# A softmax attention in periods of two key tiles, with values in three blocks, maxima in single banks, and every eighth unit of maxima folded by GpSimd

## The chip, the cores and the metric

The kernel runs on one core of a Trainium2 chip. The metric is the device time of one execution in microseconds (us); smaller is better. Five engines share the work: TensorE (PE in the profile, its weight loads PEld), VectorE (DVE), ScalarE (ACT), GpSimd (POOL), and SyncE (SP), which issues most DMAs.

## What is computed

Two transformer layers over 2 x 2048 tokens of width 256. Softmax attention with 16 heads of 16 stands in layer 0 and again in the last part of layer 1; between them lie a mixture of experts and a linear attention. The change touches softmax attention alone:

```python
q, k, v = x @ W_q.T, x @ W_k.T, x @ W_v.T          # each (B, L, 16 heads, 16); rope on q and k in layer 0
scores = einsum('blhd,bshd->bhls', q, k) / sqrt(16)
weights = softmax(scores, axis=-1)                  # over the 2048 keys
out = einsum('bhls,bshd->blhd', weights, v)
```

In layer 1 the same `softmax(q @ k.T) @ v` is computed from `x @ W_qkv + b_qkv`, and the result of the experts is added to it.

## The kernel before

`softmax_attention` is called twice; each call is one stage of the kernel. A stage goes through 32 **groups** (2 batches x 4 groups of four heads x 4 pieces of 512 queries; `n` counts them), so there are 64 groups in all. A group goes through 16 tiles of 128 keys (`u`). For each key tile and each of the four heads TensorE forms a **score** (128 keys x 512 queries, contraction over 50 rows) into one of `SB` = 3 PSUM banks (L835), ScalarE takes the exponential of it into `probs` (L905), and TensorE multiplies that with the values, 17 columns for each head, into `o_ps` (L850). The four heads' value products stand in four column strips of the array and run side by side; each is recorded as two MATMULs. The last of the 17 columns is the sum by which the result is divided.

So that the exponential doesn't overflow, every query's maximum score is needed before its group begins. It is a row of q itself (the shift rows), so it must be there ahead. For that TensorE forms the scores a second time, turned over (128 queries x 512 keys, L823, `maximum`), in **units** of one PSUM bank. VectorE reduces two units at once (L924, `max_take`, 128x1024 to 128x2) into `part_max`. There are 64 units in a group. They run `LEAD` = 8 key tiles ahead of the group that they are for. When all are there, four small steps on VectorE (`row_maxima`, L278 to L291) make the row that SP stores and loads into q.

A score reads rows 0 to 49 or 64 to 113 of the array, by the head, and a unit of maxima reads the other half: such a **pair** of score and maximum runs side by side. TensorE's order is written out by hand. In a key tile it is twice this **round**: a block of values of 256 columns for the tile before, then a pair, then a second pair. At `u` = 1 the first block is put off, which makes a run of four pairs and then 512 columns of values, so that VectorE has time to turn the finished result out of `o_ps` (`turn_result`, L930). `divide` (L934, L938) follows at `u` = 2.

The engines are tied by counting semaphores. Score c waits for exponential c-3. A pair of maxima waits until its two banks (of 2 x 2) were reduced. A block of values waits for the tile's four exponentials. The exponentials of a tile wait for the values of two tiles earlier, since `probs` has two buffers. Within one engine everything is in order.

GpSimd zeroes a DRAM buffer in the first stage (ten DMAs, after the first group). In the second it gathers the experts' rows with 64 indirect DMAs (L780), weighs and adds them (L786 to L793), and adds the finished rows (L800, L802). SP loads queries and keys ahead and stores results.

## Time and profile before

| what | value |
|---|---|
| median of 3 runs | 3513.06 us (3509.66 to 3520.32) |
| profiled execution, its own time | 3515.13 us |
| its span, first to last instruction | 3513.4 us |
| mean granted TensorE clock | 0.969 of full |
| PE busy | 3376.8 us (96%) |
| DVE busy | 3031.7 us (86%) |
| ACT busy | 2546.2 us (72%) |
| POOL busy | 514.1 us (15%) |
| the two attention stages | from 180 to 1446 us and from 2236 to about 3500 us of the span |

Busy time counts an instruction from its start to its end. The next one on the same engine can start before the end of the one ahead, so on DVE and ACT the distance between starts in a row of waiting work (called pitch below) is shorter than the duration, and an engine that reads 100% busy may still have room.

### The profile page before, as it was taken

How to read it: one execution, taken by the hardware profiler on the slowest of the kernel's cores; microseconds unless marked ns; L12 is line 12 of the kernel's file. 1: busy time of each engine (PE TensorE's matmuls, PEld its weight loads, DVE VectorE, ACT ScalarE, POOL GpSimd, SP SyncE). 2: the span in 40 equal slices, each digit the busy share in tenths (PEclk: the TensorE clock that was granted, in tenths of full speed). 3: DMA queues.
4: the chain of work that ended last, by engine and by line, in shares of the span. 5: the costliest groups of instructions: out<-in, count | busy, mean ns of one | idle time of the engine just before them, and what ended most of it. 6: DMA issues, size and time to landing. Idle time of an engine off the chain costs nothing. (4 is left out here: it accounts for less than half of the span.)

```text
span 3513.4 us, 74309 instructions
## 1 busy us (share of the span) xinstructions
PE 3376.8 (96%) x29745; PEld 1550.6 (44%) x29746; DVE 3031.7 (86%) x3971; ACT 2546.2 (72%) x4700; POOL 514.1 (15%) x405
## 2 busy tenths in 40 slices
PE   8999999999999999878999889999999999999998
PEld 5533333333333333567777657533333333333333
DVE  8889999999999998364787565599999999999992
ACT  4178888888888888533333224688888888888887
POOL 4410000000000000053321142155410010000001
PEclk9689999999999999989999989999999999999999
DMA  8451220202021200335010385513121231203001
GB/s 268 131 163 25 34 39 15 43 17 39 15 39 28 32 14 6 126 132 187 28 33 12 128 256 182 133 42 64 44 44 29 42 63 27 43 16 39 15 18 46
DMA packets 306962, 233.29 MB, mean 66 GB/s; under 512 B 205592, under 2 KB 257721, under 8 KB 301971
## 3 DMA queue, kind: packets, MB, share of 16 engines
q1 hardware_dynamic: 290308, 179.45, 22.3%
q0 software_dynamic: 14832, 47.79, 4.1%
q8 instruction: 221, 3.62, 0.5%
q10 hardware_dynamic: 1504, 1.64, 0.1%
q14 instruction: 97, 0.79, 0.1%
HBM read 126.49 MB, written 102.76 MB: 65 GB/s over the span
## 5 line engine op out<-in xcount | busy, mean ns | idle before, releaser
L905 ACT ACTIVATE att_l_probs<-att_l_s_ps 128x512 f32<-128x512 f32 x4096 | 2214.6, 595 | 312.1 <-PE att_l_s_ps L835 246.8
L924 DVE TENSOR_REDUCE att_in_part_max<-att_l_max_ps 128x2 f32<-128x1024 f32 x1952 | 2327.5, 1217 | 13.7 <-PE att_l_max_ps L823 13.1
L850 PE MATMUL att_l_o_ps<-att_l_probs,att_l_v_sb 128*17 128x256 f32 x16384 | 1273.6, 386 | 2.9 <-DMA att_l_v_sb<-v_rows 1.6
L835 PE MATMUL att_l_s_ps<-att_in_q_sb,att_in_k_sb 50*128 50x512 f32 x2048 | 759.8, 447 | 9.0 <-DVE att_l_o_ps L941 9.0
L835 PE MATMUL att_l_s_ps<-att_in_q_sb,att_l_k_sb 50*128 50x512 f32 x2048 | 741.5, 448 | 0.1
L823 PE MATMUL att_l_max_ps<-att_l_k_sb,att_in_q_sb 50*128 50x512 f32 x2048 | 725.4, 444 | 0.7 <-DVE att_in_part_max L924 0.7
L823 PE MATMUL att_l_max_ps<-att_in_k_sb,att_in_q_sb 50*128 50x512 f32 x1856 | 666.5, 449 | 0.8 <-DVE att_in_part_max L924 0.8
L850 PEld LDWEIGHTS att_l_o_ps<-att_l_probs,att_l_v_sb 128*17 128x17 f32 x16384 | 278.6, 95 | 724.6 <-issue 382.9
L835 PEld LDWEIGHTS att_l_s_ps<-att_in_q_sb,att_in_k_sb 50*128 50x128 f32 x2048 | 312.2, 186 | 443.9 <-ACT att_l_probs L905 415.7
L835 PEld LDWEIGHTS att_l_s_ps<-att_in_q_sb,att_l_k_sb 50*128 50x128 f32 x2048 | 307.7, 184 | 434.1 <-ACT att_l_probs L905 397.2
L823 PEld LDWEIGHTS att_l_max_ps<-att_l_k_sb,att_in_q_sb 50*128 50x128 f32 x2048 | 291.2, 184 | 6.9 <-DVE att_in_part_max L924 6.9
L823 PEld LDWEIGHTS att_l_max_ps<-att_in_k_sb,att_in_q_sb 50*128 50x128 f32 x1856 | 266.6, 186 | 6.7 <-DVE att_in_part_max L924 6.5
L1175 POOL MEMSET post_ones<- 128x128 bf16 x1 | 0.2, 205 | 1217.8 <-POOLq L71 1217.8
L800 POOL TENSOR_TENSOR att<-att,all_gates 128x1024 f32<-128x1024 f32 x7 | 16.6, 2375 | 852.4 <-DMA att<-att_rows 852.4
L930 DVE STREAM_TRANSPOSE att_l_o_sb<-att_l_o_ps 128x512 f32<-128x512 f32 x64 | 45.2, 706 | 102.2 <-PE att_l_o_ps L850 102.2
L1736 ACT ACTIVATE lin_o_sb<-lin_o_ps 128x512 f32<-128x512 f32 x32 | 19.1, 598 | 99.3 <-PE lin_o_ps L1631 99.3
L780 POOL DMA_INDIRECT att_l_got<-tile_out,all_get_at x64 | 64.6, 1010 | 152.7 <-ACT att_l_probs L905 149.6
L1820 DVE TENSOR_TENSOR lin_masked<-lin_qk_ps,all_triu 128x1024 f32<-128x1024 f32 x64 | 75.2, 1217 | 9.6 <-PE lin_qk_ps L1622 9.6
L266 DVE TENSOR_REDUCE att_in_part_max<-ffn_qk_ps 128x2 f32<-128x1024 f32 x48 | 56.5, 1217 | 30.6 <-PE ffn_qk_ps L257 30.6
L2108 PE MATMUL ffn_v_ps<-ffn_w_exp,ffn_hT 128*128 x320 | 82.1, 385 | 0.0
L2015 POOL DMA_INDIRECT slot_rows<-ffn_z_all,all_get_at x64 | 62.8, 981 | 96.0 <-DVE all_get_at L2282 77.1
L1178 POOL DMA_INDIRECT slot_rows<-next_z_all,post_put_at x64 | 62.5, 976 | 86.1 <-DVE all_get_at L1472 68.1
(262 smaller groups left out, 2778.7 us busy)
## 6 DMA issues: line engine op xcount, KB each, us to landing
att_in_q_sb<-q_hi SPq DMA_DIRECT2D x256, 64.0 KB
slot_rows<-att_l_zeros POOLq DMA_DIRECT2D x10, 1024.0 KB, 15.7
ffn_parts<-slot_rows SPq DMA_DIRECT2D x40, 256.0 KB, 3.1
tile_out<-ffn_parts SPq DMA_DIRECT2D x40, 256.0 KB, 2.2
att_in_q_sb<-q_lo SPq DMA_DIRECT2D x128, 72.0 KB
att_l_v_sb<-v_rows SPq DMA_DIRECT2D x16, 544.0 KB, 15.9
att_in_k_sb<-k_hi SPq DMA_DIRECT2D x32, 256.0 KB, 9.1
att_l_k_sb<-k_hi SPq DMA_DIRECT2D x32, 256.0 KB, 10.0
```

The lines of the kernel that those rows point to most:

```text
L266: nc.vector.reduce_max(ai.part_max[:, k // MAXI, k % MAXI], ps[:, k % 2 * 2:k % 2 * 2 + 2], AX.X).then_inc(ai.slot_taken, 1)
L780: nc.gpsimd.indirect_dma_start(out=got[:, k, t], out_offset=None, in_=io.tile_out, in_offset=bass.IndirectOffsetOnAxis(ap=m.get_at[:, b, k ...
L823: ins = nc.tensor.matmul(max_ps[:, r, half], q_sb[rows, j % QR, pair, tile * P:(tile + 1) * P], k_sb[j // GPB % 2][rows, pair, part * G:(p ...
L835: nc.tensor.matmul(s_ps[:, c % SB], k_sb[j // GPB % 2][rows, pair, u * P:(u + 1) * P], q_sb[rows, j % QR, pair], start=True, stop=True).th ...
L850: last = nc.tensor.matmul(o_ps[32 * h:32 * h + AUG, cols], v_sb[:, j // GPB % 2, u, h * AUG:(h + 1) * AUG], probs[:, u % 2, h, cols], star ...
L905: nc.scalar.activation(probs[:, u % 2, h], s_ps[:, c % SB], ACT.Exp, scale=float(HD) ** -0.5).then_inc(exp_done, 1)
L924: nc.vector.reduce_max(part_max[:, j % 2, k], max_ps[:, r], AX.X).then_inc(slot_taken, 1)
L930: nc.vector.transpose(o_sb[:].rearrange("p k c -> p (k c)"), o_ps[:]).then_inc(o_copied, 1)
L1178: nc.gpsimd.indirect_dma_start(out=io.slot_rows, out_offset=bass.IndirectOffsetOnAxis(ap=put_at[:, b, k, t:t + 1], axis=0), in_=m.z_all[:, ...
L1820: nc.vector.tensor_tensor(masked[:, t % 2, banks].rearrange("p r e n -> p (r e) n"), qk_ps[:, banks].rearrange("p r (e n) -> p (r e) n", n=P),
L2015: nc.gpsimd.indirect_dma_start(out=io.slot_rows, out_offset=bass.IndirectOffsetOnAxis(ap=m.get_at[:, b, k, t:t + 1], axis=0), in_=z_all[:, ...
L2108: last = nc.tensor.matmul(out_ps[:, i % 2, t], slot_hT[:, i % 2, kh, t * P:(t + 1) * P], w_exp[:, kh, ds(experts[t] * D, D)], start=False, ...
```

## The change

- **Periods.** Two key tiles make a period (`w`, 8 in a group). In it TensorE does 8 pairs and three blocks of values in place of four: 3 pairs, values 0:320 of the tile before; 2 pairs, its values 320:512; 3 pairs, values 0:512 of the period's first tile. Period 0 of a group has two blocks of 512 columns, behind 3 and behind 5 pairs. `probs` gets a third buffer (`PB`).
- **Maxima in single banks.** The eight units of a period go through four single banks. VectorE takes units 0, (1, 2), 3, 4 and (5, 6): three reduces of one bank and two of two banks.
- **Unit 7 by another way.** ScalarE copies it from PSUM to SBUF behind the period's eight exponentials (L959, `unit_sb`). GpSimd folds its upper half onto the lower (L779 to L783: high minus low, maximum with 0, plus low) into `folded`, 256 wide. VectorE reduces four folded units at once (L993, `take_folds`), twice in a group: in period 4 and in period 5, each time behind unit 0. The four steps of `row_maxima` follow in period 5, `divide` moves to period 1.
- **GpSimd's other work** is now interleaved with the folds, one piece a period.

Core of the diff (the new helpers `zero_rows`, `gather`, `add_experts`, `add_result` hold the loops' old bodies and are left out):

```diff
+PB = 3
+STEP_TILES = 2
+STEPS_G = KT // STEP_TILES
+UNITS = 4 * STEP_TILES
+MB = 4
+TAKES = ((0,), (1, 2), (3,), (4,), (5, 6))
+COPIED = UNITS - 1
+HB = 4
+FOLDED = MAXI // GPB
+ROUNDS = ((3, 0, 320), (2, 320, 512), (3, 0, 512))
+RESULT_STEP, ROWMAX_STEP = 1, LEAD // STEP_TILES + 1
-        max_ps = pb("max_ps", [P, 2, 2, G])
+        max_ps = pb("max_ps", [P, MB, G])
...
+            def reduce_unit(p):
+                g, k, half = unit_of(p // STEPS_G, p % STEPS_G, COPIED)
+                pool.wait_ge(unit_copied, p + 1)
+                low, high = unit_sb[:, p % HB, 0:G // 2], unit_sb[:, p % HB, G // 2:G]
+                nc.gpsimd.tensor_tensor(high, high, low, ALU.subtract).then_inc(fold_step, 1)
+                pool.wait_ge(fold_step, 2 * p + 1)
+                nc.gpsimd.tensor_scalar(high, high, 0.0, None, ALU.max).then_inc(fold_step, 1)
+                pool.wait_ge(fold_step, 2 * p + 2)
+                nc.gpsimd.tensor_tensor(folded[:, g % 2, k // GPB], low, high, ALU.add).then_inc(unit_reduced, 1)
...
+                behind, held = divmod(UNITS * p + i - MB, UNITS)
+                if behind >= 0:
+                    if held == COPIED:
+                        pe.wait_ge(unit_copied, behind + 1)
+                    else:
+                        pe.wait_ge(units_taken, behind * len(TAKES) + TAKE_OF[held] + 1)
...
+                    for r, (count, c0, c1) in enumerate(ROUNDS):
+                        products(n, w, pair, count)
+                        pair += count
+                        values(n, STEP_TILES * w - (r < 2), c0, c1)
...
+            def copy_unit(p):
+                act.wait_ge(unit_ready, UNITS * p + COPIED + 1)
+                if p >= HB:
+                    act.wait_ge(unit_reduced, p - HB + 1)
+                nc.scalar.activation(unit_sb[:, p % HB], max_ps[:, COPIED % MB], ACT.Copy).then_inc(unit_copied, 1)
...
+            for n in range(STEPS):
+                for w in range(STEPS_G):
+                    for t in range(len(TAKES)):
+                        take_units(n, w, t)
+                        if w == ROWMAX_STEP - 1 and t == 0 and 0 < n < STEPS - 1:
+                            take_folds(n + 1, 0)
+                        if w == ROWMAX_STEP and n + 1 < STEPS:
+                            if t == 0:
+                                take_folds(n + 1, 1)
+                                dve.wait_ge(folds_taken, 2 * n + 1)
+                                dve.wait_ge(units_taken, period_of(n, LEAD // STEP_TILES) * len(TAKES))
+                            else:
+                                row_maxima(nc, dve, ai, n + 1, n + 1, t - 1, FIRST)
```

How this moves the work on two engines. First TensorE, before, in the middle of a group of the first stage: two key tiles (`att_l0_s_ps` is a score, `att_l0_max_ps` a unit of maxima, `att_l0_o_ps` the values).

```order
L850 MATMUL att_l0_o_ps<-att_l0_probs,att_l0_v_sb 17x256 x4
L835 MATMUL att_l0_s_ps<-att_in0_q_sb,att_in0_k_sb0 128x512
L823 MATMUL att_l0_max_ps<-att_in0_k_sb0,att_in0_q_sb 128x512 x2
L835 MATMUL att_l0_s_ps<-att_in0_q_sb,att_in0_k_sb0 128x512
L850 MATMUL att_l0_o_ps<-att_l0_probs,att_l0_v_sb 17x256 x4
L835 MATMUL att_l0_s_ps<-att_in0_q_sb,att_in0_k_sb0 128x512
```

The same engine after the change, one whole period:

```order
L895 MATMUL att_l0_s_ps<-att_in0_q_sb,att_in0_k_sb0 128x512
L885 MATMUL att_l0_max_ps<-att_in0_k_sb0,att_in0_q_sb 128x512 x2
L895 MATMUL att_l0_s_ps<-att_in0_q_sb,att_in0_k_sb0 128x512 x2
L885 MATMUL att_l0_max_ps<-att_in0_k_sb0,att_in0_q_sb 128x512
L910 MATMUL att_l0_o_ps<-att_l0_probs,att_l0_v_sb 17x320 x4
L885 MATMUL att_l0_max_ps<-att_in0_k_sb0,att_in0_q_sb 128x512
L895 MATMUL att_l0_s_ps<-att_in0_q_sb,att_in0_k_sb0 128x512 x2
L885 MATMUL att_l0_max_ps<-att_in0_k_sb0,att_in0_q_sb 128x512
L910 MATMUL att_l0_o_ps<-att_l0_probs,att_l0_v_sb 17x192 x4
```

TensorE now goes from pairs to values and back three times in two key tiles, and not four times.

VectorE before, where a group's row maxima are made, up to where the result is turned:

```order
L278 TENSOR_REDUCE att_in0_row_max<-att_in0_part_max 128x8 x2
L924 TENSOR_REDUCE att_in0_part_max<-att_l0_max_ps 128x2
L282 CAST att_in0_max_parts<-att_in0_row_max 128x16
L924 TENSOR_REDUCE att_in0_part_max<-att_l0_max_ps 128x2
L285 TENSOR_TENSOR att_in0_max_parts<-att_in0_row_max,att_in0_max_parts 128x16
L924 TENSOR_REDUCE att_in0_part_max<-att_l0_max_ps 128x2
L291 STREAM_TRANSPOSE att_in0_max_cols<-att_in0_max_parts 128x32
L924 TENSOR_REDUCE att_in0_part_max<-att_l0_max_ps 128x2 x13
L930 STREAM_TRANSPOSE att_l0_o_sb<-att_l0_o_ps 128x512
```

VectorE after, from the first take of a group's period 5 to the first of period 6 (L984 takes units, L993 folded units; another L993 stands in the same place of period 4):

```order
L984 TENSOR_REDUCE att_in0_part_max<-att_l0_max_ps 128x1
L993 TENSOR_REDUCE att_in0_part_max<-att_l0_folded 128x4
L984 TENSOR_REDUCE att_in0_part_max<-att_l0_max_ps 128x2
L278 TENSOR_REDUCE att_in0_row_max<-att_in0_part_max 128x8 x2
L984 TENSOR_REDUCE att_in0_part_max<-att_l0_max_ps 128x1
L282 CAST att_in0_max_parts<-att_in0_row_max 128x16
L984 TENSOR_REDUCE att_in0_part_max<-att_l0_max_ps 128x1
L285 TENSOR_TENSOR att_in0_max_parts<-att_in0_row_max,att_in0_max_parts 128x16
L984 TENSOR_REDUCE att_in0_part_max<-att_l0_max_ps 128x2
L291 STREAM_TRANSPOSE att_in0_max_cols<-att_in0_max_parts 128x32
L984 TENSOR_REDUCE att_in0_part_max<-att_l0_max_ps 128x1
```

A reduce of folded units, 4 x 256 elements long, now stands in front of the take that the row maxima follow, and the four small steps lie behind single takes and not 16 tiles' even pairs.

## Rows read from the trace of the kernel before

**Rows 1.** The page, part 1: busy time of each engine and its instructions

```profile
PE 3376.8 (96%) x29745; PEld 1550.6 (44%) x29746; DVE 3031.7 (86%) x3971; ACT 2546.2 (72%) x4700; POOL 514.1 (15%) x405
```

**Rows 2.** Busy time by stretch, first stage: PE, PEld, DVE, ACT, POOL, clock, DMA

```profile
208.00:1370.00 1162.00, 1162.00 (x11334) 422.01 (x11332) 1160.65 (x1182) 1022.04 (x1889) 5.36 (x10) 1.00 0.19 35
```

**Rows 3.** L930 alone, one a group, in two stretches: durations in ns, starts

```profile
L930 DVE STREAM_TRANSPOSE att_l_o_sb<-att_l_o_ps x30: 705/705/707, 229.5 to 1371.8; 128x512 f32<-128x512 f32 x30
...
L930 DVE STREAM_TRANSPOSE att_l_o_sb<-att_l_o_ps x3: 707/717/718, 1371.8 to 1444.1; 128x512 f32<-128x512 f32 x3
```

**Rows 4.** Timeline of PE in a steady round: start us, us, engine, line

```profile
712.25 0.63 PE L850 MATMUL att_l_o_ps<-att_l_probs,att_l_v_sb 128*17 128x256 f32 x8
712.81 0.49 PE L835 MATMUL att_l_s_ps<-att_in_q_sb,att_l_k_sb 50*128 50x512 f32 x1
...
713.14 0.38 PE L835 MATMUL att_l_s_ps<-att_in_q_sb,att_l_k_sb 50*128 50x512 f32 x1
713.47 0.63 PE L850 MATMUL att_l_o_ps<-att_l_probs,att_l_v_sb 128*17 128x256 f32 x8
```

**Rows 5.** Timeline at a group's tile 1: four pairs, then 512 columns of values

```profile
699.78 2.45 DVE L924 TENSOR_REDUCE att_in_part_max<-att_l_max_ps 128x2 f32<-128x1024 f32 x2
...
701.46 0.50 PE L835 MATMUL att_l_s_ps<-att_in_q_sb,att_l_k_sb 50*128 50x512 f32 x1
...
701.80 0.62 PE L835 MATMUL att_l_s_ps<-att_in_q_sb,att_l_k_sb 50*128 50x512 f32 x2
...
702.28 0.49 PE L823 MATMUL att_l_max_ps<-att_l_k_sb,att_in_q_sb 50*128 50x512 f32 x2
...
703.13 1.06 PE L850 MATMUL att_l_o_ps<-att_l_probs,att_l_v_sb 128*17 128x256 f32 x16
...
704.12 0.49 PE L835 MATMUL att_l_s_ps<-att_in_q_sb,att_l_k_sb 50*128 50x512 f32 x1
```

**Rows 6.** Timeline of ACT: two exponentials back to back

```profile
709.59 1.08 ACT L905 ACTIVATE att_l_probs<-att_l_s_ps 128x512 f32<-128x512 f32 x2 [0.21 <-PE att_l_s_ps L835]
```

**Rows 7.** Timeline of DVE around a group's result

```profile
820.32 0.70 DVE L930 STREAM_TRANSPOSE att_l_o_sb<-att_l_o_ps 128x512 f32<-128x512 f32 x1
820.95 4.58 DVE L924 TENSOR_REDUCE att_in_part_max<-att_l_max_ps 128x2 f32<-128x1024 f32 x4
825.46 0.23 DVE L934 RECIPROCAL att_l_inv<-att_l_o_sb 128x16 f32<-128x16 f32 x1
...
826.07 4.61 DVE L924 TENSOR_REDUCE att_in_part_max<-att_l_max_ps 128x2 f32<-128x1024 f32 x4
```

**Rows 8.** Timeline of DVE around the row maxima

```profile
800.81 0.27 DVE L278 TENSOR_REDUCE att_in_row_max<-att_in_part_max 128x8 f32<-128x32 f32 x2
801.00 1.22 DVE L924 TENSOR_REDUCE att_in_part_max<-att_l_max_ps 128x2 f32<-128x1024 f32 x1
802.13 0.17 DVE L282 CAST att_in_max_parts<-att_in_row_max 128x16 fp32r<-128x16 f32 x1
```

**Rows 9.** Timeline of PE behind a `divide`: score, then its late unit

```profile
630.31 0.49 PE L835 MATMUL att_l_s_ps<-att_in_q_sb,att_in_k_sb 50*128 50x512 f32 x1
...
630.46 0.58 PE L823 MATMUL att_l_max_ps<-att_l_k_sb,att_in_q_sb 50*128 50x512 f32 x2
```

**Rows 10.** Groups of instructions on POOL: count, then busy us and mean ns

```profile
L448 POOL TENSOR_TENSOR qkv_parts<-qkv_whole,qkv_parts 128x512 fp32r<-128x512 f32 x32 | 40.1, 1276 | 54.4 <-ACT qkv_parts L535 54.4
...
L457 POOL TENSOR_SCALAR qkv_prod<-qkv_prod 128x1024 f32<-128x1024 f32 x2 | 5.6, 2785 | 0.2
```

**Rows 11.** Timelines of DVE and of POOL in the second stage, row maxima

```profile
2418.07 0.27 DVE L278 TENSOR_REDUCE att_in_row_max<-att_in_part_max 128x8 f32<-128x32 f32 x2
...
2420.81 1.42 DVE L285 TENSOR_TENSOR att_in_max_parts<-att_in_row_max,att_in_max_parts 128x16 fp32r<-128x16 f32 x1
...
2417.34 2.39 POOL L788 TENSOR_TENSOR att_l_got<-att_l_got 128x1024 f32<-128x1024 f32 x1
2419.80 2.39 POOL L790 TENSOR_TENSOR att_l_got<-att_l_got,all_gates 128x1024 f32<-128x1024 f32 x1
```

More of the change, by code:

```diff
@@ new lines, in _ @@
+            for p in range(PERIODS):
+                reduce_unit(p)
+                if zero_slots and ZERO_STEP <= p < ZERO_STEP + B * ROWS_B * D // P // ZEROS:
+                    zero_rows(p - ZERO_STEP)
+                if last and 1 <= p <= B * GPB * (GATHERS + ADDS):
+                    i, s = divmod(p - 1, GATHERS + ADDS)
+                    if s < GATHERS:
+                        gather(i, s)
+                    else:
+                        add_experts(i, s - GATHERS)
+                if last:
+                    for i in range(RESULTS):
+                        if p - ADD_AT[i] in (0, 1):
+                            add_result(i, p - ADD_AT[i])
@@ L821, in maximum @@
+                behind, held = divmod(UNITS * p + i - MB, UNITS)
+                if behind >= 0:
+                    if held == COPIED:
+                        pe.wait_ge(unit_copied, behind + 1)
+                    else:
+                        pe.wait_ge(units_taken, behind * len(TAKES) + TAKE_OF[held] + 1)
                 pair, tile, part = maximum_parts(k)
                 rows = slice(half * HROWS, half * HROWS + XROWS)
[L823 to L824 removed]
@@ L825, in maximum @@
-                if half == 0:
-                    ins.then_inc(slot_ready, 1)
+                nc.tensor.matmul(max_ps[:, i % MB], q_sb[rows, j % QR, pair, tile * P:(tile + 1) * P],
+                                 k_sb[j // GPB % 2][rows, pair, part * G:(part + 1) * G], start=True, stop=True).then_inc(unit_ready, 1)
             def scores(n, j, u, h):
@@ L897, in _, with products @@
-            for part in range(2):
-                values(STEPS - 1, NB - 1, KT - 1, NIT - 1, part)
+            def products(n, w, first, count):
+                for pair in range(first, first + count):
+                    row, second = divmod(pair, 2)
+                    c = 2 * row + second
+                    u, h = STEP_TILES * w + c // HG, c % HG
+                    if second:
+                        maximum(n, w, c)
+                        scores(n, n % NB, u, h)
+                    else:
+                        scores(n, n % NB, u, h)
+                        maximum(n, w, c)
@@ L916, in _ @@
+            for n in range(STEPS):
+                for u in range(KT):
+                    for h in range(HG):
+                        if h == 0 and n * KT + u >= PB:
+                            act.wait_ge(pv_done, n * KT + u - PB + 1)
+                        exps(n, u, h)
+                    if u % STEP_TILES == STEP_TILES - 1 and period_of(n, u // STEP_TILES) < PERIODS:
+                        copy_unit(period_of(n, u // STEP_TILES))
             if last:
@@ L921, in _, with take_units, take_folds @@
         def _(dve):
-            def max_take(used, r, j, k):
-                dve.wait_ge(slot_ready, used + 1)
-                nc.vector.reduce_max(part_max[:, j % 2, k], max_ps[:, r], AX.X).then_inc(slot_taken, 1)
+            def take_units(n, w, t):
+                p, units = period_of(n, w), TAKES[t]
+                if p >= PERIODS:
+                    return
+                g, k, half = unit_of(n, w, units[0])
+                first = 2 * k + half
+                dst = part_max[:, g % 2, first:first + 1] if len(units) == 1 else part_max[:, g % 2, first:first + 4:3]
+                banks = max_ps[:, units[0] % MB:units[0] % MB + len(units)]
+                dve.wait_ge(unit_ready, UNITS * p + units[-1] + 1)
+                nc.vector.reduce_max(dst, banks, AX.X).then_inc(units_taken, 1)
+            def take_folds(g, part):
+                periods = period_of(g - 1, LEAD // STEP_TILES * part)
+                dve.wait_ge(unit_reduced, periods)
+                _, k, half = unit_of(0, 0, COPIED)
+                at = slice(part * FOLDED // 2, (part + 1) * FOLDED // 2)
+                first = 2 * (GPB * at.start + k % GPB) + half
+                dst = part_max[:, g % 2, first:2 * GPB * at.stop:2 * GPB]
+                nc.vector.reduce_max(dst, folded[:, g % 2, at], AX.X).then_inc(folds_taken, 1)
             def turn_result(n):
```

213 lines of the change are left out of this document (92 added, 121 removed).

## The prediction

> **What bounds the kernel now.** I read the page first, then busy time by stretch, then the timelines of the engines in one attention stage. PE is busy for 96% of the span and DVE for 86% [rows 1]; in the first stage both are busy all the time, at the full clock [rows 2]. So the reader has to ask which of them really has no room. Thirty turns of the result lie from 229.5 to 1371.8 us: 29 groups at 39.39 us [rows 3]. A steady round on PE goes value block 712.25, first pair 712.81, second pair 713.14, next block 713.47 [rows 4]: 1.22 us, 32 of them 39.0 us. Nothing in it is late. DVE's reduce of two units takes 1.22 us, but four that had work waiting stand at a pitch of (4.58 - 1.22) / 3 = 1.12, or 1.13 with 4.61 [rows 7]. 32 at 1.13 are 36.2, and with turn (0.63), divide (0.61) [rows 7] and row maxima (0.19 for the first step, 0.07 for the second [rows 8], and I take 0.1 each for the last two, 0.46 in all) 37.9 us a group. ACT has a pitch of 1.08 - 0.59 = 0.49 us [rows 6], 64 of them 31.4. So **PE is the bound, by its own work**, DVE is 3% under it, ACT 20%.
>
> **What PE's round is made of.** A block of 256 columns takes 0.56 us up to the next pair, one of 512 without a break 703.13 to 704.12 = 0.99 [rows 4, 5]. So a column costs 0.43 / 256 = 0.0017 us and a turn from values to pairs 0.12. In the run of four pairs the first pair holds 0.34, while the third starts 0.62 - 0.39 = 0.23 behind the second [rows 5]; the last pair before values holds 0.33. A pair thus costs 0.23 inside a run, with 0.10 more at each end of it. Every turn there and back costs some 0.33 us and works on nothing.
>
> In the Trainium skill, "TensorEngine Tiling (Array Packing)", Tiling Modes, Key Properties, says that a change of tiling mode drains TensorE. The trace agrees: the 0.1 us at each change.
>
> **The change on PE.** Runs of 3, 2 and 3 pairs: 0.34 + 0.23 + 0.33 = 0.90, 0.67, 0.90, together 2.47. Blocks of 320, 192 and 512 columns: 0.12 + 0.54 = 0.66, 0.45, 0.99, together 2.10. A period is 4.55 us, against 4 x 1.22 = 4.88. 8 periods are 36.4 us, **2.6 us a group less** if nobody else is late.
>
> **The change on DVE.** A take of one unit isn't in the trace. Half of a reduce's elements are worth 1.22 - 0.70 = 0.52 (against the turn of 512 elements [rows 7]); its pitch is then 1.13 - 0.52 = 0.61, its duration 0.70. Bounds: 0.57 (half of 1.13) and 0.63 (the turn's pitch). A period: 3 x 0.61 + 2 x 1.13 = 4.09, 8 of them 32.7. A reduce of folded units reads 1024 elements from SBUF: 1.13, not below the 1.04 that two times 0.52 give. Two of them, with the old 1.7 for turn, divide and maxima, make 36.7 us a group. So the ceiling on both engines is near 36.5, and the question is what they lose to each other.
>
> **Where they meet.** Count from a period's first pair. Units 0, 1, 2 are there at 0.53, 0.77 and 1.00, unit 3 at 2.1 and 5 and 6 at 3.4. DVE starts its takes at 0.53, 1.14, 2.27, 2.88 and 3.49. From the end of a reduce to PE's start are 0.05 (699.78 + 2.45 to 702.28 [rows 5]). The take of units 1, 2 ends at 2.36, and PE wants their bank at 2.66: 0.25 to spare. That of unit 3 ends at 2.97, PE wants it at 3.23: 0.20. That of 5, 6 ends at 4.71, PE wants it at 4.55 + 0.34 = 4.89: **0.12**. DVE is then free at 4.62 and the next unit 0 comes at 5.08, so DVE idles 0.46 a period, but it can't work ahead in it. Whatever is put on DVE in a period beyond 0.12 us moves PE, if it is put behind unit 0. Before the change such a pair was wanted 0.40 after it was free (the reduce that starts at 713.57 is done at 714.79, and its banks are wanted at 713.47 + 1.22 + 0.56 = 715.25); a divide of 0.61 then held one unit up by 0.15 [rows 9].
>
> The lumps of a group:
> - Period 4: 1.13 - 0.12 = 1.01.
> - Period 5: fold 1.13, and 0.19 + 0.07 + 0.1 of the row maxima ahead of the last take: 1.49 - 0.12 = 1.37.
> - Period 1: divide, 0.61 - 0.12 = 0.49.
> - Period 0: it has one turn of PE less (4.2 us), but unit 3 is taken behind the result's turn, from 2.90 to 3.60; its bank is wanted by pair 8. That starts at 3.65, values follow at 4.0 and end at 5.0 to 5.1: 0.5 over a common period.
>
> Sum 3.4. Where PE waits inside a run of pairs its pipeline fills again, 0.1 as at a run's start: up to six places, I take 0.4. ACT has nine operations a period, 9 x 0.49 = 4.4 of 4.55 (the copy priced as an exponential of the same shape): its room falls from 20% to 3%. The next period's first exponential is 0.1 late, and pair 8, which waits for exponential 4, loses some 0.02; 0.1 a group. **36.4 + 3.4 + 0.4 + 0.1 = 40.3**, and with 0.1 for GpSimd (next) 40.4 us a group, 1.0 more than now.
>
> **GpSimd.** Two-input 512 elements take 1.28, one-input 1024 2.79 [rows 10], two-input 1024 2.39 [rows 11]: for 256 about 0.7, 0.8 and 0.7, 2.3 us a period of 4.55, in a ring of four copies; the extra work of the second stage fits beside. Nobody waits for the folds as such. But while POOL worked on SBUF, DVE's subtraction of 16 elements (L285) took 1.42 us, and ended when POOL's operation did (2419.80 + 2.39 = 2422.19), while the reduces at 2418.07 weren't longer than elsewhere [rows 8, 11]. POOL is now at work half of each period in both stages. Open to it are L282, L285 and the product in `divide`, each by at most one operation, 0 to 0.8 us; by my times the row maxima miss POOL's three operations and the product meets the last. I take 0.1 a group; 0 and 1.5 stay as ends.
>
> The Trainium skill, "GPSIMD Engine Reference", Key points, says that GpSimd shares its SBUF interfaces with VectorE and contends with instructions that have two SBUF inputs or run in a two-port mode. That rule speaks against this change: the page and the row name the same steps. It gives no price; the sum with the row's bounds would be 0 to 1.5 us a group.
>
> **The rest.** 61 groups' worth carry maxima: 61 x 1.0 = 61 us more. The last 1.5 groups of each stage have none (two groups take 1444.1 - 1371.8 = 72.3 us [rows 3]); there ACT's pitch is the floor (3.95 for a period's eight) and one turn fewer gives 0.2 to 0.5 a period: 24 periods, 8 us less. The zeroing DMAs and gathers move to other times of POOL, whose queue nobody waits for; SP's queue keeps its order. Sum: 3515 + 61 - 8 = 3568 for the profiled execution; it was 2 us over the median, so about **3565 us**.
>
> **Rivals.**
> 1. *The lumps are absorbed.* For it: the units stand in four separate banks, and 0.46 us of idle is in each period; the room of 0.12 rests on differences of rows, and if single takes cost 0.57 and the rest is 0.1 better, each of the four lumps costs 0.2 less and no refill. Against it: the idle time lies before unit 0, the lumps behind it. Wholly absorbed, DVE bounds at 36.7: 3515 - 61 x 2.7 - 8 = 3342. Half absorbed (2 us a group less than forecast) it is 38.4: 3447. A chance of 0.27.
> 2. *GpSimd's hold on SBUF* becomes the dear part: it must reach L285, L282 and the product in most groups, 1.5 us a group in place of 0.1: 3565 + 85 = 3650. It decides once POOL's three operations last beyond 3.6 us of a period. For it: the one row of 1.42; against it: POOL's pieces are now a quarter as long. 0.10.
> 3. *It comes out even:* lumps of 2.4 in place of 3.4 and all else as forecast, 39.4 a group: 3507. 0.15.
> 4. *ScalarE is the bound:* if the copy takes 0.2 us more than an exponential, a period is 4.65 at least, but waits for DVE then shrink; 0.1 a period, 0.5 a group in all: 3595. 0.08. A table load for each copy (the change not doing what it says) is out: the program has one load per stage, as before.
>
> The forecast itself, lumps between 2.9 and 4.1 a group, has 0.40, and gives 3535 to 3610.
>
> **Range and chances.** 0.3% is about what a measurement of this kernel can tell. Faster 0.27 (rival 1), same 0.15 (rival 3), slower 0.58 (forecast, 2 and 4). The range takes in the forecast, rivals 3 and 4, and the half of rival 1 down to 3440, and reaches toward rival 2 at 3625. The likeliest case's own range is 3535 to 3610.
>
> **What would show it.** PE periods of 4.55 us in periods 2, 3, 6 and 7, with blocks and runs as priced; single takes at a pitch of 0.61; gaps on PE of 0.9 before unit 5 in periods 4 and 5, released by DVE; about 40.4 us from turn to turn. It is wrong if DVE has no idle time before unit 0, if the gaps in periods 4 and 5 are under 0.5, or if steady periods differ from 4.55 by over 0.1.

## The result, and the profile after

The changed kernel takes 3609.62 us (median of 4 runs, 3608.14 to 3612.86). The kernel before took 3511.36 in the same series (4 runs, 3508.97 to 3520.32). The ratio is 1.0273, with an interval of 1.0256 to 1.0291: slower, by some 98 us where 52 were forecast, inside the range of 3440 to 3625 and at the upper edge of the likeliest case. The profiled execution is the one of 3608.14 us (span 3606.4, mean granted clock 0.97).

The page after, part 1:

```profile
PE 3325.1 (92%) x25137; PEld 1540.8 (43%) x25138; DVE 2931.1 (81%) x4581; ACT 2717.8 (75%) x5188; POOL 1646.5 (46%) x1877
```

Busy time by stretch in the first attention stage and in the second (columns as in [rows 2]):

```profile
208.00:1370.00 1162.00, 1093.63 (x8862) 402.71 (x8859) 1070.54 (x1422) 1063.94 (x2045) 530.27 (x691) 1.00 0.19 35
2236.00:3440.00 1204.00, 1127.08 (x9000) 435.47 (x8998) 1063.98 (x1406) 1080.26 (x2076) 703.81 (x793) 1.00 0.23 44
```

In [rows 1] PE was busy for 96% of the span and in [rows 2] for all of the first stage. Now it is idle for 68 us of the same 1162, DVE for 91 and ACT for 98, at the same full clock. Nobody is full: the three engines wait for each other. Who waits for whom is in the page's part 5 (busy us, mean ns, then idle time before the group and its releaser):

```profile
L984 DVE TENSOR_REDUCE att_in_part_max<-att_l_max_ps 128x1 f32<-128x512 f32 (+1 forms) x2440 | 2072.9, 896 | 200.8 <-PE att_l_max_ps L885 194.0
...
L885 PE MATMUL att_l_max_ps<-att_l_k_sb,att_in_q_sb 50*128 50x512 f32 x2048 | 728.1, 444 | 73.3 <-DVE att_in_part_max L984 70.3
...
L885 PE MATMUL att_l_max_ps<-att_in_k_sb,att_in_q_sb 50*128 50x512 f32 x1856 | 662.8, 447 | 64.2 <-DVE att_in_part_max L984 61.3
```

PE's idle time lies before the units of maxima and is ended by DVE's takes; DVE's lies before its takes and is ended by PE. The turns of the result, against [rows 3]:

```profile
L999 DVE STREAM_TRANSPOSE att_l_o_sb<-att_l_o_ps x28: 704/706/707, 267.1 to 1372.2; 128x512 f32<-128x512 f32 x28
```

(1372.2 - 267.1) / 27 = 40.93 us a group, against 39.39. To place this inside a group I took, from the records of PE, the time from one period's first score to the next one's, as a mean over 27 groups of the first stage (w is the period; a group is the sum; in the kernel before a period is two key tiles).

| us | w0 | w1 | w2 | w3 | w4 | w5 | w6 | w7 | group |
|---|---|---|---|---|---|---|---|---|---|
| before | 5.09 | 4.88 | 5.04 | 4.88 | 4.88 | 4.87 | 4.87 | 4.87 | 39.39 |
| forecast (refills and small terms apart) | 5.05 | 5.04 | 4.55 | 4.55 | 5.56 | 5.92 | 4.55 | 4.55 | 40.4 |
| after | 5.06 | 5.35 | 4.78 | 4.68 | 5.58 | 5.90 | 4.92 | 4.67 | 40.93 |

The whole difference of 93 us between the profiled executions: the 29 groups between a stage's first and thirtieth turn give 44.9 and 44.6, together 89.5; the last two groups of each stage 2 x 1.96 = 3.9; the part of a stage from its first score to its first turn -4.4 and -0.4; what lies between and around the stages 4.4.

A steady period (w7) on PE, against [rows 4]:

```profile
669.38 0.50 PE L895 MATMUL att_l_s_ps<-att_in_q_sb,att_in_k_sb 50*128 50x512 f32 x1
...
670.27 0.73 PE L910 MATMUL att_l_o_ps<-att_l_probs,att_l_v_sb 128*17 128x320 f32 x8
670.94 0.50 PE L885 MATMUL att_l_max_ps<-att_l_k_sb,att_in_q_sb 50*128 50x512 f32 x1
...
671.60 0.52 PE L910 MATMUL att_l_o_ps<-att_l_probs,att_l_v_sb 128*17 128x192 f32 x8
672.05 0.50 PE L885 MATMUL att_l_max_ps<-att_l_k_sb,att_in_q_sb 50*128 50x512 f32 x1
...
672.62 0.39 PE L885 MATMUL att_l_max_ps<-att_l_k_sb,att_in_q_sb 50*128 50x512 f32 x1
672.64 0.50 PE L895 MATMUL att_l_s_ps<-att_in_q_sb,att_in_k_sb 50*128 50x512 f32 x1
673.07 1.05 PE L910 MATMUL att_l_o_ps<-att_l_probs,att_l_v_sb 128*17 128x512 f32 x8
674.05 0.49 PE L895 MATMUL att_l_s_ps<-att_in_q_sb,att_l_k_sb 50*128 50x512 f32 x1
```

Read the starts. The first run of three pairs takes 670.27 - 669.38 = 0.89, the block of 320 columns 0.67, the run of two 0.66, the block of 192 0.45, the long block 0.98: all as priced. Only the second run of three takes 1.02 in place of 0.90. Its last score starts a little behind its unit of maxima (672.64, not 672.62), and the values follow 0.43 behind it and not 0.33. What that score waits for stands under experiment 4.

The timeline of DVE around the folds of periods 4 and 5, then that of PE in period 4 (in brackets the idle time before and its releaser):

```profile
653.56 0.69 DVE L984 TENSOR_REDUCE att_in_part_max<-att_l_max_ps 128x1 f32<-128x512 f32 x1 [0.53 <-PE att_l_max_ps L885]
654.16 1.21 DVE L993 TENSOR_REDUCE att_in_part_max<-att_l_folded 128x4 f32<-128x1024 f32 x1
655.29 3.54 DVE L984 TENSOR_REDUCE att_in_part_max<-att_l_max_ps 128x2 f32<-128x1024 f32 x4
659.14 0.69 DVE L984 TENSOR_REDUCE att_in_part_max<-att_l_max_ps 128x1 f32<-128x512 f32 x1 [0.31 <-PE att_l_max_ps L885]
659.75 1.21 DVE L993 TENSOR_REDUCE att_in_part_max<-att_l_folded 128x4 f32<-128x1024 f32 x1
```

```profile
655.21 0.52 PE L910 MATMUL att_l_o_ps<-att_l_probs,att_l_v_sb 128*17 128x192 f32 x8
656.56 0.50 PE L885 MATMUL att_l_max_ps<-att_l_k_sb,att_in_q_sb 50*128 50x512 f32 x1 [0.83 <-DVE att_in_part_max L984]
```

DVE idles 0.53 us, takes unit 0, then reads the folded units for 655.29 - 654.16 = 1.13, and only then starts on units 1 and 2. PE has no room for unit 5 until they are read: 655.21 to 656.56 is 1.35 where 0.45 is the usual.

Period 6 holds no fold and still lasts 4.92. Its second pair waits for the take of units 5 and 6 of period 5, which the small steps of the row maxima have made late:

```profile
663.68 1.21 DVE L984 TENSOR_REDUCE att_in_part_max<-att_l_max_ps 128x2 f32<-128x1024 f32 x1
664.95 0.72 PE L895 MATMUL att_l_s_ps<-att_in_q_sb,att_in_k_sb 50*128 50x512 f32 x2
```

The take ends at 664.89 and the pair starts at 664.95, 0.48 behind the first one (664.47) where 0.34 is the usual: 0.14 of waiting, and 0.10 until PE is back at its pace, since the third pair follows 0.34 later and not 0.23.

### The profile page after: what moved, and what is told of

Same layout as the page of the kernel before. It is cut to its first block and busy times, and to the rows that moved or that the text cites. A ratio compares the mean times of both kernels' runs of the same rounds, so it can differ in the third digit from the quotient of the medians.

```text
span 3606.4 us, 68202 instructions
## 1 busy us (share of the span) xinstructions
PE 3325.1 (92%) x25137; PEld 1540.8 (43%) x25138; DVE 2931.1 (81%) x4581; ACT 2717.8 (75%) x5188; POOL 1646.5 (46%) x1877
## 5 line engine op out<-in xcount | busy, mean ns | idle before, releaser
L952 ACT ACTIVATE att_l_probs<-att_l_s_ps 128x512 f32<-128x512 f32 x4096 | 2158.2, 598 | 229.4 <-PE att_l_s_ps L895 206.5
L984 DVE TENSOR_REDUCE att_in_part_max<-att_l_max_ps 128x1 f32<-128x512 f32 (+1 forms) x2440 | 2072.9, 896 | 200.8 <-PE att_l_max_ps L885 194.0
L910 PE MATMUL att_l_o_ps<-att_l_probs,att_l_v_sb 128*17 128x512 f32 (+2 forms) x11776 | 1169.5, 469 | 1.1 <-DMA att_l_v_sb<-v_rows 1.0
L779 POOL TENSOR_TENSOR att_l_unit_sb<-att_l_unit_sb 128x256 f32<-128x256 f32 x488 | 358.4, 734 | 1081.4 <-ACT att_l_unit_sb L959 1080.9
L885 PEld LDWEIGHTS att_l_max_ps<-att_l_k_sb,att_in_q_sb 50*128 50x128 f32 x2048 | 330.2, 184 | 379.8 <-DVE att_in_part_max L984 202.8
L781 POOL TENSOR_SCALAR att_l_unit_sb<-att_l_unit_sb 128x256 f32<-128x256 f32 x488 | 413.0, 846 | 42.8
L910 PEld LDWEIGHTS att_l_o_ps<-att_l_probs,att_l_v_sb 128*17 128x17 f32 x11776 | 195.1, 95 | 462.0 <-issue 427.1
L783 POOL TENSOR_TENSOR att_l_folded<-att_l_unit_sb 128x256 f32<-128x256 f32 x488 | 356.5, 731 | 40.6
L959 ACT ACTIVATE att_l_unit_sb<-att_l_max_ps 128x512 f32<-128x512 f32 x488 | 301.1, 617 | 0.0
L993 DVE TENSOR_REDUCE att_in_part_max<-att_l_folded 128x4 f32<-128x1024 f32 x122 | 147.7, 1211 | 5.4 <-POOL att_l_folded L783 5.4
```

The costliest lines, as they stand in the source:

```text
L779: nc.gpsimd.tensor_tensor(high, high, low, ALU.subtract).then_inc(fold_step, 1)
L781: nc.gpsimd.tensor_scalar(high, high, 0.0, None, ALU.max).then_inc(fold_step, 1)
L783: nc.gpsimd.tensor_tensor(folded[:, g % 2, k // GPB], low, high, ALU.add).then_inc(unit_reduced, 1)
L885: nc.tensor.matmul(max_ps[:, i % MB], q_sb[rows, j % QR, pair, tile * P:(tile + 1) * P], k_sb[j // GPB % 2][rows, pair, part * G:(part + 1 ...
L910: last = nc.tensor.matmul(o_ps[32 * h:32 * h + AUG, c0:c1], v_sb[:, j // GPB % 2, u, h * AUG:(h + 1) * AUG], probs[:, (n * KT + u) % PB, h ...
L952: nc.scalar.activation(probs[:, (n * KT + u) % PB, h], s_ps[:, c % SB], ACT.Exp, scale=float(HD) ** -0.5).then_inc(exp_done, 1)
```

## Experiments

All times are of the first attention stage unless said otherwise. Four runs stand beside one run of the kernel before of 3522.02 us (the first four here), the rest beside 3515.76 (median of 9), the last beside 3513.83. Experiments 5 and 6 were run five times, the others once, so a difference of some 10 us between their totals says little; the times of the periods say more.

**1. Folds made small.** VectorE reads 16 of each 256 folded elements; the number and places of its instructions stay. What is left out is most of the folded values.

```diff
-                nc.vector.reduce_max(dst, folded[:, g % 2, at], AX.X)
+                nc.vector.reduce_max(dst, folded[:, g % 2, at, 0:16], AX.X)
```

> Edit: VectorE's two reduces of folded units read 4 x 16 elements in place of 4 x 256, so part of the keys is left out of the row maxima; everything else as in the changed kernel (40.91 us a group). Theory A (what is put on DVE behind a period's unit 0 moves PE, because DVE can't use its idle time ahead of unit 0): the two folds of 1.13 us cost PE about 1.0 us each and 0.1 to 0.2 of refill, so a group takes 38.6 to 38.9 us, the time is 3470 to 3490 us, and period 4 is as long as period 3 (4.68 us in place of 5.58). Theory B (ScalarE's ninth operation and GpSimd's hold on SBUF set the time, the folds lie in DVE's idle time): within 0.2 us of 40.9 a group, 3600 us.

Measured: 3510.61 us, 39.03 a group, both longer than expected. Period 4 went from 5.58 to 4.68, period 5 from 5.90 to 4.90, all others stayed. The reduce went from 1211 to 211 ns (DVE's instructions by form):

```profile
L993 DVE TENSOR_REDUCE att_in_part_max<-att_l_folded 128x4 f32<-128x64 f32 x57 | 12.0, 211 | 0.0
```

1.0 us less on DVE gave 0.91 and 0.99 of PE's time. So the two folds, where they stood, are what made the kernel slower: without them it stands at the kernel before. In the second stage a group took 39.59, though its median periods are those of the first stage; five of its periods 6 last 6.9 to 9.7 us, of the kind shown at experiment 5.

**2. Folds moved behind the period's last take.** Nothing is left out.

```diff
+                        if w == ROWMAX_STEP - 3 and t == len(TAKES) - 1 and 0 < n < STEPS - 1:
+                            take_folds(n + 1, 0)
+                        if w == ROWMAX_STEP - 1 and t == len(TAKES) - 1 and n + 1 < STEPS:
+                            take_folds(n + 1, 1)
```

> Edit: the same two reduces of folded units, at full size, stand behind the last take of periods 2 and 4 in place of behind the first take of periods 4 and 5. DVE's work is the same to the element. Theory A: behind the last take DVE has its idle time of about 0.5 us, so a fold makes it late by 0.6 and PE by 0.3 to 0.5, not 1.0: 39.6 to 40.0 us a group, 3530 to 3555 us. Theory C (DVE's summed work decides, wherever it stands): no change, 40.9 a group, 3608 us.

Measured: 3541.77 us, 39.60 a group, as theory A said; w3 is 4.94, w4 4.76, w5 5.12. The fold now begins when DVE would have gone idle:

```profile
642.22 4.20 DVE L984 TENSOR_REDUCE att_in_part_max<-att_l_max_ps 128x1 f32<-128x512 f32 x5 [0.31 <-PE att_l_max_ps L885]
646.34 1.21 DVE L993 TENSOR_REDUCE att_in_part_max<-att_l_folded 128x4 f32<-128x1024 f32 x1
647.46 1.81 DVE L984 TENSOR_REDUCE att_in_part_max<-att_l_max_ps 128x1 f32<-128x512 f32 x2
```

A group is 0.57 us longer than with the shrunken folds of experiment 1, where it was 1.90 longer with the folds behind unit 0. The gap before unit 0 is real room, and the place decides what a step on DVE costs.

**3. One folded unit a period.** Eight reduces of 256 elements, each behind its period's last take.

```diff
+                        if t == 4 and 0 < period_of(n, w) <= PERIODS:
+                            take_fold(period_of(n, w) - 1)
```

> Edit: each folded unit is reduced by itself (128x256), one in every period, behind the last take; eight reduces of 256 elements in place of two of 1024. DVE's work rises by eight fixed parts of some 0.07 us. Theory A: a reduce of 256 elements has a pitch of 0.33 us, less than the idle 0.5, so the folds cost PE nothing: 38.6 to 38.9 us a group, as with the folds shrunk, 3470 to 3490 us; that would be below the kernel before. Theory C: 8 x 0.07 = 0.5 us a group more, 41.4, 3640 us.

Measured: 3490.76 us, 38.77 a group; w4 and w5 are both 4.68, w6 4.89. The group is as expected, the total 1 us over. Shortest, median and longest duration of the folds:

```profile
L990 DVE TENSOR_REDUCE att_in_part_max<-att_l_folded x488: 395/407/421, 194.1 to 3421.2; 128x1 f32<-128x256 f32 x163
```

Eight reduces hold DVE longer than two (its busy time is 2934.2 against 2931.1 us), and the profiled execution is 117 us shorter. This is the cut of the work that fits the gap.

**4. The cut of the values at 288.** ROUNDS becomes (3, 0:288), (2, 288:512), (3, 0:512).

> Edit: the values of the second tile are cut 0:288 and 288:512, not 0:320 and 320:512; so scores 3 and 4 start 0.05 us earlier, and the period's other work stands still. Theory D (the steady period of 4.67 us, forecast 4.55, is 0.12 too long since pair 8's score waits for exponential 4, some 0.03 us, and the pipeline that runs dry costs 0.1 more): periods 3 and 7 fall to 4.56 to 4.60, a group to 40.2 to 40.6 us, 3565 to 3590 us. Rival (ScalarE's nine operations at their pitch fill the period, 9 x 0.49 = 4.4 and its waits): periods 3 and 7 stay at 4.67, 3608 us.

Measured: 3593.59 us, 40.83 a group; the steady periods are 4.62, 0.05 less where 0.08 to 0.12 were expected. On PE, the last run of three in a steady period:

```profile
671.36 0.50 PE L885 MATMUL att_l_max_ps<-att_l_k_sb,att_in_q_sb 50*128 50x512 f32 x1
...
671.93 0.39 PE L885 MATMUL att_l_max_ps<-att_l_k_sb,att_in_q_sb 50*128 50x512 f32 x1
672.33 1.05 PE L910 MATMUL att_l_o_ps<-att_l_probs,att_l_v_sb 128*17 128x512 f32 x8
```

The run takes 0.97 now, between 1.02 and 0.90. What is left of the wait shows in the weight loads of this run (PEld):

```profile
671.47 0.45 PEld L885 LDWEIGHTS att_l_max_ps<-att_l_k_sb,att_in_q_sb 50*128 50x128 f32 x2
671.90 0.18 PEld L895 LDWEIGHTS att_l_s_ps<-att_in_q_sb,att_in_k_sb 50*128 50x128 f32 x1
```

In the changed kernel the last one stands at:

```profile
672.64 0.18 PEld L895 LDWEIGHTS att_l_s_ps<-att_in_q_sb,att_in_k_sb 50*128 50x128 f32 x1
```

The last score waits for exponential 4, the period's fifth. Counted from the period's start, as means over 27 groups, this exponential ends at 3.16 (3.21 in the changed kernel), the score's weights are loaded at 3.21 (3.26), and the unit beside it has had its own since 3.04 in both. The score now starts together with its unit (3.24 both), and the values still follow 0.40 behind it: 0.43 in the changed kernel, 0.33 in a run that waits for nothing. So the exponential moved with the scores by the full 0.05, and the period with it. The load stays 0.17 late, and of the 0.12 there is 0.07 left, which goes with this late load and not with a pair that starts apart. A cut still earlier, which would test that, wasn't run.

This run's mean contains two disturbed groups (18 and 24), each 1.3 us longer at a granted clock of 0.50; the median periods add up to 40.70 a group, against 40.90 in the changed kernel.

**5. Experiments 3 and 4 together, with the small steps put last.** The reciprocal goes behind the last take of period 1, the product behind that of period 2.

```diff
+                        if n > 0 and w == 1 and t == len(TAKES) - 1:
+                            invert(n - 1)
+                        if n > 0 and w == 2 and t == len(TAKES) - 1:
+                            scale_result(n - 1, n - 1)
```

> Edit: as the kernel with one folded unit a period (38.77 us a group in the first stage, 3490.8 us), and the values' cut at 288, and the divide taken apart: the reciprocal behind the last take of period 1, the product behind that of period 2, where GpSimd's three operations are over. Theory A (idle time of DVE lies between the last take and the next unit 0, some 0.5 us, and steps that fit there are free): the 0.8 us that periods 1 and 2 lose to the divide fall to 0.2, the product takes 0.43 in place of 0.69 us, the cut gives 0.05 in five periods: 37.6 to 38.1 us a group, 3405 to 3445 us, below the kernel before by 2 to 3%. Rival (the divide's lump is only moved: recovered elsewhere, 3.3% of work is work): 38.6 to 38.8 us a group, 3480 us.

Measured in five rounds: 3432.71 us (3426.99 to 3443.62), a ratio to the kernel before of 0.9771 (0.9752 to 0.9790), so 2.3% faster. A group is 37.84: 5.06, 4.70, 4.68, 4.62, 4.63, 4.64, 4.88, 4.62. DVE in periods 0 to 2:

```profile
612.45 0.41 DVE L990 TENSOR_REDUCE att_in_part_max<-att_l_folded 128x1 f32<-128x256 f32 x1
612.78 0.24 DVE L1000 RECIPROCAL att_l_inv<-att_l_o_sb 128x16 f32<-128x16 f32 x1
613.02 4.15 DVE L984 TENSOR_REDUCE att_in_part_max<-att_l_max_ps 128x1 f32<-128x512 f32 x5
617.08 0.41 DVE L990 TENSOR_REDUCE att_in_part_max<-att_l_folded 128x1 f32<-128x256 f32 x1
617.41 0.41 DVE L1006 TENSOR_TENSOR att_l_o_div<-att_l_o_sb,att_l_inv 128x256 f32<-128x256 f32 x1
617.74 4.14 DVE L984 TENSOR_REDUCE att_in_part_max<-att_l_max_ps 128x1 f32<-128x512 f32 x5
```

The steps follow each other without a gap, and PE doesn't wait for them beyond 0.1. Period 6 keeps its 4.88: the small steps of the row maxima still stand ahead of a take.

In the second stage 29 groups take 1113.6 us against 1097.7 in the first. The median periods are the same; four periods 6 last 8.08, 9.77, 8.87 and 6.05 us. Just ahead of each, L285, a step of the row maxima, is held by one of GpSimd's operations for the experts (1.33 to 1.82 us in place of 0.16). In the longest:

```profile
2441.44 2.37 POOL L813 TENSOR_TENSOR all_x_res<-all_x_res,att_l_got 128x1024 f32<-128x1024 f32 x1
2442.04 1.81 DVE L285 TENSOR_TENSOR att_in_max_parts<-att_in_row_max,att_in_max_parts 128x16 fp32r<-128x16 f32 x1
```

Busy time by stretch there (columns as in [rows 2]):

```profile
2443.00:2445.00 2.00, 0.07 (x2) 0.00 (x0) 2.00 (x3) 0.83 (x2) 1.91 (x3) 1.00 0.01 4
2445.00:2449.00 4.00, 3.96 (x24) 1.20 (x24) 3.22 (x6) 2.05 (x4) 2.24 (x3) 0.52 0.15 38
```

The take of units 5 and 6 comes late by the hold, PE is busy for 0.07 of 2 us, and in the four behind them its granted clock is 0.52, near the lower level of 1.2 GHz. The period loses 4.9 us for a hold of 1.7. Three of the four long periods have such a stretch. This is the hold that rival 2 of the prediction is about; with what follows it, it costs some 16 us in this version.

**6. The turn one take later,** behind unit 3 and no longer ahead of it, on top of experiment 5 (`t == 2` for `t == 1`).

> Edit: as e5_small_steps_last, with the turn of the result behind the take of unit 3 and not in front of it. Theory A: unit 3's bank is free 0.6 us earlier and pair 8 no longer waits for it, but then waits for exponential 4, so period 0 falls by 0.1 us or less, from 5.05; 6 us less in all than e5_small_steps_last. Rival: the values behind it wait for the turn, which ends 0.6 us later, period 0 grows by up to 0.3 us, 18 us more.

Measured in five rounds: 3444.31 us (3438.40 to 3450.55), 0.9802 (0.9785 to 0.9819). w0 fell by 0.07 to 4.99, as the early wait for unit 3 says, but w1 rose by 0.18 to 4.88. The step's time came back in the next period, and more of it: neither expectation had that. A group is 0.11 longer in the first stage (37.95) and 0.02 in the second; of the 11 us between the two profiled executions 7.5 lie outside the attention stages. So the move gains nothing, and it costs some 3 us rather than 11.

**7. GpSimd made short.** It subtracts and clamps 16 elements and copies the lower half, so that the upper half of unit 7 is left out. (Of the diff, one of three such lines.)

```diff
-                nc.gpsimd.tensor_tensor(high, high, low, ALU.subtract).then_inc(fold_step, 1)
+                tiny = high[:, 0:16]
+                nc.gpsimd.tensor_tensor(tiny, tiny, low[:, 0:16], ALU.subtract).then_inc(fold_step, 1)
```

> Edit to the changed kernel: GpSimd copies only the lower half of the unit (128x256, one input) and does two steps of 16 elements, in place of three operations of 256; the other half of every eighth unit is left out of the maxima. POOL's chain in a period falls from 2.45 to some 1.3 us; nothing else is changed. Theory E (the divide's product, 0.69 us in place of 0.42, is held by GpSimd's third operation, and that moves PE): the product is back at 0.42 to 0.43, periods 1 and 2 together fall by 0.25, group 40.65 us, 3590 us. Rival (the product is longer for another reason, its place behind the reciprocal): it stays at 0.69, 3608 us.

Measured: 3608.60 us. First, from the timeline of the changed kernel, the product of `divide` and GpSimd beside it:

```profile
640.47 0.73 POOL L783 TENSOR_TENSOR att_l_folded<-att_l_unit_sb 128x256 f32<-128x256 f32 x1
...
640.80 0.69 DVE L1007 TENSOR_TENSOR att_l_o_div<-att_l_o_sb,att_l_inv 128x256 f32<-128x256 f32 x1
```

All 64 products there (shortest, median, longest in ns), and those of this experiment (208 to 1330 us, busy us and mean ns):

```profile
L1007 DVE TENSOR_TENSOR att_l_o_div<-att_l_o_sb,att_l_inv x64: 424/694/740, 231.4 to 3592.0; 128x256 f32<-128x256 f32 x64
```

```profile
L1008 DVE TENSOR_TENSOR att_l_o_div<-att_l_o_sb,att_l_inv 128x256 f32<-128x256 f32 x27 | 11.5, 425 | 0.9
```

With GpSimd out of the way the product is back at its 425 ns, and w1 fell by 0.27 to 5.08: the expected mechanism. The median periods add up to 40.63 us a group in the first stage and 40.64 in the second, against 40.90 in both: theory E's 40.65. It doesn't show in the total, since single groups lose it again. In the second stage GpSimd's sums for the experts now meet the product: five products last 1.56 to 2.04 us, each until 0.28 after such an operation (the longest from 2613.65 to 2615.69, beside a POOL L809 that ends at 2615.41). Behind that one PE waits, its granted clock is 0.50 from 2618 to 2626, and the group's periods 1 to 3 are 5.9 us longer. A group of the second stage is 41.36 us in the mean, against 41.02 in the changed kernel. In the first stage period 5 of two groups runs into a stretch at 0.50 and is 0.86 longer, which is most of the 0.07 by which the mean of w5 rose (to 5.96); why it came there isn't settled.

**8. The three blocks without the copy and the folds.** Eight units in four takes of two, straight from PSUM; nothing is left out.

```diff
-TAKES = ((0,), (1, 2), (3,), (4,), (5, 6))
+TAKES = ((0, 1), (2, 3), (4, 5), (6, 7))
-COPIED = UNITS - 1
+COPIED = -1
```

> Edit to the changed kernel: three blocks of values and the third buffer of exponentials stay, but the eight units of a period are taken by VectorE in four reduces of two banks, as before the change, without copy and folds. DVE's work is that of the kernel before, 37.9 us a group; PE's own is 36.4. Theory F (who waits is decided by when a bank comes free, not by sums): pair 5 of a period waits for units 0, 1 (0.15 us), pair 7 for 2, 3 (0.2), the next pair 3 for 6, 7 (0.25), each with a refill of 0.1: a period of 5.1 to 5.3 us, 41 to 43 us a group, 3610 to 3720 us, slower than the full change. Rival G (saved turns count by themselves; DVE at 37.9 bounds): 38 to 39 us a group, 3430 to 3490 us, and then copy and folds were the mistake.

Measured: 3770.36 us, 43.37 a group, no mean period under 5.16: theory F's direction, and more than it expected. Its last run of three pairs on PE:

```profile
671.23 0.50 PE L887 MATMUL att_l_max_ps<-att_l_k_sb,att_in_q_sb 50*128 50x512 f32 x1
671.24 0.72 PE L897 MATMUL att_l_s_ps<-att_in_q_sb,att_in_k_sb 50*128 50x512 f32 x2
671.95 0.50 PE L887 MATMUL att_l_max_ps<-att_l_k_sb,att_in_q_sb 50*128 50x512 f32 x2
...
672.60 1.05 PE L912 MATMUL att_l_o_ps<-att_l_probs,att_l_v_sb 128*17 128x512 f32 x8
```

The run takes 1.37. The second pair's score runs at once, its unit of maxima has no bank until 671.95, and the two no longer run side by side. So the single banks and the copy together weren't the mistake: without them this run of three comes apart. Which of the two is needed isn't separated.

**9. The end of a stage.** On top of experiment 5, periods without maxima go back to four rounds of two scores and 256 columns.

```diff
+HALVES = ((2, 0, 256), (2, 256, 512), (2, 0, 256), (2, 256, 512))
+                    rounds = ROUNDS if period_of(n, w) < PERIODS else HALVES
```

> The last version (folds one unit at a time, blocks of 288, 224 and 512, small steps behind last takes), with one edit: in the periods that form no maxima (12 at the end of each stage) TensorE goes back to the old rounds of two pairs and a block of 256 values, four a period. No computation is left out. Those periods measure 4.61 us in the last version and 4.44 in the kernel before, though the last version changes array modes less often. Theory H (without maxima the loop from score to exponential and back is the limit; a run of three scores uses up the three score banks and a block of 512 values leaves ScalarE without a score, so runs and blocks of equal size keep it fed): 4.43 to 4.47 a period, about 2 us less in each stage, some 3428 us in all. Rival I (the third buffer of exponentials, or the place of the result's turn, makes these periods longer): 4.58 to 4.62 as before the edit, 3432 us. Rival J (TensorE's own work is the limit there, so that a fourth change of modes costs): 4.8 or more, 3437 us.

Measured: such a period is 4.44 us against 4.61, in both stages. ACT in the changed kernel in such a period, and in this experiment:

```profile
1463.75 4.12 ACT L952 ACTIVATE att_l_probs<-att_l_s_ps 128x512 f32<-128x512 f32 x8 [0.49 <-PE att_l_s_ps L895]
```

```profile
1371.81 5.53 ACT L954 ACTIVATE att_l_probs<-att_l_s_ps 128x512 f32<-128x512 f32 x10
```

With the long block ACT runs dry once a period; with equal blocks it doesn't. PE's runs of three scores in the changed kernel, in the period from 1463.16:

```profile
1463.16 0.73 PE L895 MATMUL att_l_s_ps<-att_in_q_sb,att_l_k_sb 50*128 50x512 f32 x3
1465.77 1.09 PE L895 MATMUL att_l_s_ps<-att_in_q_sb,att_l_k_sb 50*128 50x512 f32 x3
```

The same three scores take 0.66 up to the values once (1463.82) and 1.02 the other time (1466.79): the turn that was saved comes back as waiting. The first period of the last group is 0.3 longer (5.03 against 4.71), once, so a stage gains 1.1 us where 2 were expected (in the first, from its turn 30 to its turn 32: 73.41 to 72.29). The total of 3432.38 us in one run tells nothing of so small a step.

## Why the prediction was right, and where it was off

**PE's own work: mostly right, and the largest error of the sum.** Runs, blocks and turns came out within 0.02 us, but for the last run. The period is 4.67 and not 4.55, so the term of 36.4 should have been 37.4 a group. Part of that, 0.02 a period, is a slip: the prediction's own 2.47 and 2.10 add up to 4.57. The rest is the last run: it takes 0.12 more than priced, the other runs and blocks together 0.02 less. The prediction saw that the last score waits for exponential 4 and gave it 0.02 a period; it left out that the values behind the score come late as well, 0.43 behind it and not 0.33. Together that is 1.0 us a group. It is also one of the prediction's three signs of being wrong: steady periods over 0.1 from 4.55 (periods 3 and 7 at 4.68 and 4.67; periods 2 and 6, listed as steady, at 4.78 and 4.92). The other two signs didn't come: DVE idles before unit 0, and the gap in period 4 is 0.83 (periods 4 and 5 are 0.91 and 1.22 longer than a steady one).

**DVE and the lumps: right in kind and place, a little high in size.** Single takes last 0.68 and stand at 0.60 (653.56 to 654.16); the fold holds 1.13; DVE idles before unit 0 (0.53 above, 0.46 forecast). Against the real steady period of 4.675, periods 4, 5, 0, 1, 2 and 6 are longer by 0.91, 1.22, 0.38, 0.67, 0.11 and 0.24: 3.5, where lumps, refills, ACT and GpSimd were put at 4.0. The room is as counted, the waits inside a run cost the 0.10 of a refill, and part of period 5's lump falls into period 6. A longer steady period gives DVE more room in each, so that the two errors partly cancel. Experiments 1 and 2 confirm mechanism and place. That the time of 3609.62 still lies inside the likeliest case is partly luck: the difference to the kernel before is 98 us and not 52, and the upper edge is 3610.

**GpSimd's hold: right step, wrong size.** Forecast 0.1 a group, with the guess that GpSimd's last operation may meet the product. It met it in 60 of 64 groups, for 0.27 us each. The row maxima were missed in the first stage (L285 174 ns at most), as forecast; in the second, L282 was held five times, up to 1.21 us, and those periods 6 are 0.5 to 1.1 us longer. The kernel is close to losing more there, as experiments 1, 5 and 7 show, where steps that are held last 1.3 to 2.3 us, most of them with a stretch at the lower granted clock behind; neither the forecast nor rival 2 had that.

**The rest: wrong sign.** The last groups of the stages were to give 8 us back and cost 3.9. The step that failed is "one turn fewer gives 0.2 to 0.5 a period". It took ACT's pitch as the floor (3.95) and a turn as pure gain. But a period took 4.44 there before, 0.5 over that floor: the exponentials stand at (5.53 - 0.6) / 9 = 0.55 in the row of experiment 9, not at 0.49. Experiment 9 gave the fourth turn back and a period fell from 4.61 to 4.44: the spacing of the scores matters there, not the number of PE's turns.

The first group of the first stage gained 4.4 us that nobody had counted. Busy time by stretch (columns as in [rows 2]), before and then after:

```profile
190.00:200.00 10.00, 10.00 (x68) 3.32 (x64) 6.19 (x6) 5.43 (x10) 0.00 (x0) 0.60 1.07 118
```

```profile
190.00:200.00 10.00, 10.00 (x86) 3.91 (x88) 8.65 (x11) 9.34 (x20) 4.50 (x7) 0.96 1.04 113
```

The stage begins at 180 us with the granted clock at 0.50 in both, its lower level of 1.2 GHz. Before, it stays low for most of this stretch, after it is at 0.96, nearly the 2.4 GHz. In both kernels PE had been at work since the stage's start (busy for 8.23 of the 9.80 us up to 190 before, 7.57 of 8.80 after). Why it rose earlier wasn't tried; experiment 5 has 0.71 in the same stretch.

**Rivals.** Absorbed lumps (1) is out: the room is before unit 0 and the folds stood behind it. Moved into it, they are absorbed, which is what experiments 3 and 5 did; that experiment 5's 3432.71 us is near the 3447 of that rival's half is chance, as it is another kernel. GpSimd (2) takes 0.27 of its 1.5 in this kernel. Lumps of 2.4 (3) are out at 3.5. ScalarE (4) wasn't the bound: the copy lasts 0.617 against 0.598 for an exponential, not 0.2 more. But the last score's wait for exponential 4 makes the last run 0.12 longer.

## What to carry to other kernels

Before moving work onto an engine with idle time, find where in the period that time lies and put the work right ahead of the wait, in pieces no longer than the gap: the same folds cost 1.9 us a group behind unit 0 and next to nothing behind the last take in eight pieces. Count the room from the other engine's next claim, and price a wait by what it delays behind it as well as by its length. A cycle of fewer, larger blocks saved its turns where the engine was bound by its own work; where TensorE fed ScalarE through three banks, even spacing won (4.44 against 4.61). And look at single long periods as well as at means: in experiments 1, 5 and 7 a few of them, all but two in the second stage, cost 16 to 20 us.
